# The last steps of a layer-norm, block-FP4 FFN and long-convolution kernel: one silu moved ahead of two squares, and four output tiles handed between engines

## The chip, the cores and the metric

The kernel runs on one NeuronCore of a Trainium2 chip. Its engines are TensorE (PE, matmuls and transposes), VectorE (DVE), ScalarE (ACT), GpSimd (POOL) and SyncE (SP, which only issues transfers). The metric is the device time of one execution in microseconds (us), lower is better. An execution is "faster" or "slower" here only beyond a few tenths of a per cent of about 588 us.

## The reference

The input `u` has 8 sequences of 1024 rows of 256 channels. What is computed is

```python
xn = layernorm(x)                      # x = u, over the 256 channels
s  = causal convolution of xn with a 128-tap kernel per channel + xn * D
gate = fp4(xn) @ fp4(w_gate).T         # 256 -> 704, blocks of 16 share a scale
y    = fp4(xn) @ fp4(w_up).T
h    = silu(gate) * y
g    = silu(fp4(h) @ fp4(w_down).T)    # 704 -> 256
out  = x + s * g
```

where `fp4` rounds every block of 16 to eight magnitudes times the block's own scale and multiplies back.

## The kernel before, in words

The 8192 rows are 64 tiles (NT) of 128 rows, worked two at a time: a pair of tiles is a step, and there are NP = 32 steps. For each tile PE multiplies the normalised input with the gate and up weights (`gate_up`, L1224), ACT takes the silu of the gate half (`silu_gate`, L615), DVE multiplies it with the up half (`h_mult`, L883). One step later DVE, ACT and POOL quantise the pair's 2 x 704 values of `h`: DVE finds block maxima (L785 or L799), scales (L818), ACT squares (`square`, L630), DVE rounds twice (`round_a` L852, `round_b` L857) and multiplies with the split scales (`h_parts`, L891, semaphore `hl_v`). PE then transposes the rounded tile (`h_transpose`, L1233), ACT copies it out of PSUM (`h_copy`, L610, semaphore `hT_a`), PE multiplies it with the down weights (`down`, L1242 and L1244), and ACT takes the last silu into `gbuf` (`silu_out`, L619, semaphore `g_a`). `down` of a tile waits until the `silu_out` two tiles earlier has been done (`after(pe, g_a, n)`), since both use the same half of a PSUM bank.

The convolution runs on PE between the FFN's matmuls in the steps 8 to 29; its result lies in `yv`, the place of the tensor `xh`. The output is `gbuf * yv + u`. Up to tile 55, POOL multiplies (`gated`, L516, in three parts of the channels per four tiles: one of 128 x 512 elements and two of 128 x 256) and sends the product with an accumulating DMA (`add_out`, L520) into `out`, into which SP has copied `u` beforehand (`copy_input`). The last eight tiles are handled at the end: DVE multiplies the six tiles 56 to 61 at once (L1143), POOL sends them with one accumulating DMA, and for tiles 62 and 63 DVE multiplies (L1143) and adds `u` from an SBUF buffer `u_last` (L1152), and SP stores each with a plain DMA (L453).

All engines run lists written out by hand in program order, with semaphores between engines; nothing is scheduled automatically. Around the end the lists are: ACT ends with `step(NP, ...)`, that is `h_copy(60)`, the two squares of the last pair, `silu_out(59)`, `h_copy(61)`, `silu_out(60)`, `down_scale(31)`, and then `silu_out(61)`, `h_copy(62)`, `h_copy(63)`, `silu_out(62)`, `silu_out(63)`. PE ends with transposes of 60, `down(59)`, transposes of 61, `down(60)`, `down(61)`, transposes of 62 and 63, `down(62)`, `down(63)`. DVE ends with the quantisation of tiles 62 and 63, one after the other (`pieces`), and the output multiplications. The kernel's last waits are SP's for its stores and POOL's for its accumulating DMAs.

Of the kernel before, what the change touches and what calls it, by code (L numbers as in the profile page):

```python
# [12 lines left out]
ALU = mybir.AluOpType  # L13
# [4 lines left out]
P = 128  # L18
SEQS, LSEQ, H = 8, 1024, 256
NT = SEQS * LSEQ // P  # L20
NP = NT // 2
# [48 lines left out]
def build(nc, u, u_rev, D, Lre, Lim, logdt, Wre, Wim, wg, wu, wd, out):  # L70
    kpad = nc.dram_tensor("kpad", (H, 2, 3 * P), F16)
    u_t = u.rearrange("s l h -> (s l) h").rearrange("(t p) h -> p t h", p=P)
    urev = u_rev.rearrange("t p h -> p t h")
    out_t = out.rearrange("s l h -> (s l) h").rearrange("(t p) h -> p t h", p=P)

    with ExitStack() as ctx:
        ctx.enter_context(nc.allow_non_contiguous_dma(reason="a small load of D"))

        def sb(name, shape, dt):
            return ctx.enter_context(nc.sbuf_tensor(name, shape, dt))  # L80

        def sem(name):
            return ctx.enter_context(nc.semaphore(name))

        xh = sb("xh", [P, NQ, 2, NT, C2], F16)
        gbuf = sb("gbuf", [P, NT, H], F32)
# [12 lines left out]
        def carve(words):  # L99
            used[0] += words  # L100
            assert used[0] <= 14336
            return work[:, used[0] - words:used[0]]
# [4 lines left out]
        tpl_words = [carve(4 * 2 * P) for _ in range(2)]  # L107
# [7 lines left out]
        xT_words = carve(4 * H)  # L115
        xT = [xT_words[:, 2 * H * i:2 * H * (i + 1)].bitcast(F16).rearrange("p (t c k) -> p t c k", t=2, c=4) for i in range(2)]
        xin = [v[:, 2 * I:].rearrange("p (t h) -> p t h", t=2) for v in vb]
        u_last = carve(2 * H).rearrange("p (t h) -> p t h", t=2)
        by_blk = [v.rearrange("p (c k) -> p c k", k=BLK) for v in vb]
        d_bf, r_f16 = (rbuf.bitcast(dt).rearrange("p (c k) -> p c k", k=BLK) for dt in (BF16, F16))  # L120

# [98 lines left out]
        cv_h = sem("cv_h")  # L220
# [14 lines left out]
        g_a = sem("g_a")  # L235
        o_in = sem("o_in")
        f_p = sem("f_p")
        f_l = sem("f_l")
        f_y = sem("f_y")
        f_t = sem("f_t")  # L240
        f_st = sem("f_st")
        u_in = sem("u_in")
        f_out = sem("f_out")
# [118 lines left out]
            return groups_before(it + 1) - groups_before(it)  # L362

        PEEL = 4
        FIRST = NT // 4 - 2
        OPEN = [min(it for it in range(NP) if groups_before(it + 1) >= q1 * C2 // G8) for q0, q1 in PARTS]

        @block.sync
        def _(sp):
            def load_x(p, par):  # L370

                after(sp, x_r, p - 1)
                sp.dma_start(xin[1 - par], u_t[:, bass.ds(p * 2, 2), :]).then_inc(x_in[par], 16)

            sp.dma_start(dt, bass.AP(logdt.tensor, logdt.offset, [[0, P], [1, H]])).then_inc(s_small, 16)
            for m, w in enumerate((Lre, Lim)):
                dst = (lre, lim)[m]
                for half in range(2):
                    sp.dma_start(dst[64 * half:64 * half + 64, :], w.rearrange("(n o) -> n o", o=1)).then_inc(s_small, 16)
            for m, w in enumerate((Wre, Wim)):  # L380
                for half in range(2):
                    sp.dma_start(wn[:, m, :, 64 * half:64 * half + 64],
                                 w.rearrange("(t p) n -> p t n", p=P)).then_inc(s_wn, 16)
            sp.wait_ge(s_const, 2)
            sp.dma_start(dk[0:P:FA, :], D.rearrange("(o g) -> o g", g=16)).then_inc(s_d, 16)
            for m, w in enumerate((wg, wu)):
                base = wraw[:, m * RW:(m + 1) * RW].rearrange("p (t k) -> p t k", k=H)
                sp.dma_start(base[:, 0:RT - 1, :], w[0:(RT - 1) * P, :].rearrange("(t p) k -> p t k", p=P)).then_inc(s_w, 16)
                sp.dma_start(base[0:I - (RT - 1) * P, RT - 1, :], w[(RT - 1) * P:I, :]).then_inc(s_w, 16)
            sp.dma_start(wraw[:, 2 * RW:].rearrange("p (t i) -> p t i", t=2),  # L390
                         wd.rearrange("(t p) i -> p t i", p=P)).then_inc(s_w, 16)
            for i in range(4):

                sp.dma_start(gbuf[:, 16 * i:16 * i + 16, :], urev[:, 16 * i:16 * i + 16, :]).then_inc(s_xa[i], 16)
            for p in range(2):
                load_x(p, p)

            sp.wait_ge(k_zero, 1)
            for lo in (0, 2 * P - 1):
                w = P - 1 if lo == 0 else P  # L400
                sp.dma_start(kpad.ap()[:, :, lo:lo + w].rearrange("(p a) b i -> p (a b) i", p=P),
                             zero.bitcast(F16).rearrange("p (r i) -> p r i", i=P)[:, :, 0:w]).then_inc(k_pad, 16)

            load_x(2, 0)
            sp.dma_start(u_last, u_t[:, NT - 2:NT, :]).then_inc(u_in, 16)

            def store_filter():
                sp.wait_ge(k_split, 2)
                for part, src in enumerate((kh, kl)):
                    for a in range(8):  # L410
                        sp.dma_start(
                            bass.AP(kpad, part * 3 * P + P - 1 + 16 * a, [[16 * 6 * P, 16], [6 * P, 16], [1, 16]]),
                            src[a:P:FA, :].rearrange("p (g b) -> p g b", b=16)).then_inc(k_dram, 16)

            def load_t(n, par):

                after(sp, cv_h, n - 1)
                sp.dma_start(tpl[par], bass.AP(kpad, n * (4 * 6 * P), [[1, P], [3 * P, 8], [1, 2 * P]])
                             ).then_inc(t_in[par], 16)

            def copy_input(i):

                rows = LSEQ if i < SEQS - 1 else LSEQ - 2 * P
                sp.dma_start(out[i:i + 1, 0:rows], u[i:i + 1, 0:rows]).then_inc(o_in, 16)

            for it in range(PEEL):
                load_x(it + 3, (it + 1) % 2)
                if it == 2:
                    store_filter()
                copy_input(it)  # L430
            for it in range(PEEL, S_CONV):
                load_x(it + 3, (it + 1) % 2)
                copy_input(it)
            sp.wait_ge(k_pad, 32)
            sp.wait_ge(k_dram, 16 * 16)
            sp.wait_ge(w_ca, 13)
            load_t(0, 0)
            sp.wait_ge(x_hl, 2 * S_CONV + 4)
            load_t(1, 1)
            with sp.Fori(0, PAIRS - 1) as q:  # L440
                for par in range(2):
                    load_x(q * 2 + (S_CONV + par + 3), 1 - par)
                    for k in range(4 - 2 * par):
                        load_t(q * 6 + (4 * par + k + 2), k % 2)
            for it in range(S_TAIL - 2, NP - 3):
                load_x(it + 3, (it + 1) % 2)
                for n in range(2 * groups_before(it) + 2, min(2 * groups_before(it + 1) + 2, H // 4)):
                    load_t(n, n % 2)
            for n in range(2 * groups_before(NP - 3) + 2, H // 4):
                load_t(n, n % 2)  # L450
            for n in range(2):
                sp.wait_ge(f_t, n + 1)
                sp.dma_start(out_t[:, NT - 2 + n:NT - 1 + n, :], gbuf[:, NT - 2 + n:NT - 1 + n, :]).then_inc(f_st, 16)  # L453
            sp.wait_ge(f_st, 32)

        @block.gpsimd
        def _(pool):
# [60 lines left out]
            def add_out(t0, t1):  # L518

                nc.gpsimd.dma_start(out_t[:, t0:t1, :], gbuf[:, t0:t1, :], accum_op=ALU.add).then_inc(f_out, 16)  # L520
# [8 lines left out]
            for m in range(2):  # L529
                rows = uu[:, 16 + 8 * m:24 + 8 * m, :]  # L530
# [7 lines left out]

            todo = [(n, part) for n in range(FIRST) for part in range(len(PARTS))]
            made, sent = [0], [0]  # L540
# [28 lines left out]
                if it >= OPEN[0]:  # L569
                    some_gated(it, 4 if it < OPEN[2] else 8)  # L570
            some_gated(NP, NP)
            pool.wait_ge(f_l, 1)
            add_out(4 * FIRST, NT - 2)
            pool.wait_ge(f_out, 16 * (sent[0] + 1))

        @block.scalar
        def _(act):
# [124 lines left out]
            rows = [(r, r) for r in range(16)] + [(16 + r, 16 * r) for r in range(8)]  # L702
# [60 lines left out]
                step(it, it % 2, True, True, it < NP - 3, True, True, True, cv=groups_of(it), c0=groups_before(it))  # L763
            step(NP - 2, 0, False, True, False, True, True, True)
            step(NP - 1, 1, False, False, False, True, True, True)
            step(NP, 0, False, False, False, False, True, True)
            silu_out(NT - 3, 1, 0)
            for t in range(2):
                h_copy(NT - 2 + t, t, (p_hT, p_hT2)[t])
# [4 lines left out]
        def _(dve):  # L774
            own = Steps(dve, dve_n)
            V = nc.vector
# [133 lines left out]
            rows = [(r, r, 0) for r in range(16)] + [(16 + r, 16 * r, 1) for r in range(8)]  # L910
# [228 lines left out]
            def gate_y(t0, t1):  # L1139

                dve.wait_ge(g_a, t1)
                gc = by_two(gbuf[:, t0:t1, :])
                return V.tensor_tensor(gc, gc, yv[:, :, t0:t1, :].rearrange("p q t c -> p t q c"), ALU.mult)  # L1143

            dve.wait_ge(cv_e, H // G8)
            gate_y(4 * FIRST, NT - 2).then_inc(f_l, 1)
            dve.wait_ge(u_in, 16)
            for n in range(2):
                t = NT - 2 + n
                gate_y(t, t + 1).then_inc(f_y, 1)  # L1150
                dve.wait_ge(f_y, n + 1)
                V.tensor_tensor(gbuf[:, t, :], gbuf[:, t, :], u_last[:, n, :], ALU.add).then_inc(f_t, 1)  # L1152

        @block.tensor
        def _(pe):
# [186 lines left out]
```

## Time and profile before

| | us |
|---|---|
| median of 3 runs | 587.93 (586.70, 587.93, 588.83) |
| the profiled execution | 586.48 |
| its span, first to last instruction | 584.7 |
| DVE / PE / ACT / POOL busy | 544.3 / 473.7 / 407.2 / 198.4 |

Times in the rows are counted from the span's start, so 584.7 is its end. Some 1.8 us of the execution's own time lie outside the span. DVE is busy 93% of the span. The change touches only the last 25 us and some transfers; there all engines wait for each other in turn. The granted clock of TensorE (PEclk) is 1.00 at 2.4 GHz and 0.50 at 1.2 GHz.

### The profile page before, as it was taken

The page shows a single profiled execution, that of the slowest core. Times are in us where ns is not written, and L with a number is a line of the kernel's source. Part 1 is how long each engine was busy: PE and PEld are TensorE (multiplying, and loading weights), DVE is VectorE, ACT ScalarE, POOL GpSimd, SP SyncE. Part 2 cuts the span into 40 slices and gives each one's busy share as a digit, 9 for nine tenths or more (in the row PEclk, how much of TensorE's full clock was granted, in tenths as well). Part 3 has the DMA queues.
Part 4 walks back from the last instruction along what each step waited for, and adds up shares of the span by engine and source line. Part 5 has one row for each costly group of instructions (what it writes and reads, how often), then busy time and mean ns, then how long its engine had stood idle before and what let it go on. Part 6 is the DMA issues. An engine that isn't in the chain of part 4 may idle for free.

```text
span 584.7 us, 13233 instructions
## 1 busy us (share of the span) xinstructions
PE 473.7 (81%) x4956; PEld 331.3 (57%) x4956; DVE 544.3 (93%) x689; ACT 407.2 (70%) x568; POOL 198.4 (34%) x302
## 2 busy tenths in 40 slices
PE   0000356668999999999999999999999999998965
PEld 0000234225555567777777777777777777765654
DVE  6999999989999999999999999999999999998884
ACT  6972866889988876767676767676767666664552
POOL 1094000474555551111111111333333333137870
PEclk9999957989999999999999999999999999999998
DMA  5990012225222335353534353535354535339978
GB/s 173 349 281 1 1 36 90 91 27 163 91 91 91 109 83 159 102 146 108 149 105 142 112 147 103 144 111 146 104 143 114 144 107 148 110 59 154 172 104 132
DMA packets 101186, 70.80 MB, mean 121 GB/s; under 512 B 8848, under 2 KB 100752, under 8 KB 101008
## 3 DMA queue, kind: packets, MB, share of 16 engines
q1 hardware_dynamic: 93072, 61.94, 35.8%
q0 software_dynamic: 8064, 8.13, 9.5%
q8 instruction: 39, 0.64, 0.4%
q14 instruction: 11, 0.09, 0.1%
HBM read 61.28 MB, written 16.91 MB: 134 GB/s over the span
## 4 chain that ended last, share of the span: by engine, by line
PE 57%; DVE 24%; issue 9%; POOL 6%; ACT 3%; DMA 0%; SPq 0%; DVEq 0%; POOLq 0%; ACTq 0%
PE ps L1224 27%; PE ps L1242 10%; PE ps L1244 5%; PE ps L1233 5%; PE ps L1257 4%; PE ps L1261 4%; DVE wgu L944 4%; DVE work L857 2%; DVE sm L799 2%; POOL gbuf L516 2%; DVE work L883 2%; PE ps L1212 2%; DVE work L852 2%; DVE xh L919 1%; DVE xh L912 1%
## 5 line engine op out<-in xcount | busy, mean ns | idle before, releaser
L1224 PE MATMUL ps<-wgu,work 128*128 128x512 f16 (+1 forms) x1152 | 242.7, 366 | 17.1 <-DVE work L883 15.9
L1224 PEld LDWEIGHTS ps<-wgu,work 128*128 128x128 f16 x1152 | 109.9, 99 | 128.0 <-issue 17.5
L615 ACT ACTIVATE work<-ps,con 128x704 f32<-128x704 f32 x64 | 54.2, 847 | 95.1 <-PE ps L1224 95.0
L1242 PE MATMUL ps<-wdh,work 128*128 128x256 f16 x704 | 87.9, 274 | 5.5 <-ACT gbuf L619 4.7
L610 ACT COPY work<-ps 128x1408 f16<-128x1408 f16 x64 | 84.7, 1325 | 2.1 <-PE ps L1233 1.9
L852 DVE SCALAR_TENSOR_TENSOR work<-work 128x960 f32<-128x960 bf16 (+2 forms) x67 | 71.8, 1110 | 1.6 <-ACT work L630 1.5
L1242 PEld LDWEIGHTS ps<-wdh,work 128*128 128x128 f16 x704 | 65.4, 98 | 13.4 <-issue 5.3
L516 POOL TENSOR_TENSOR gbuf<-gbuf,xh 128x256 f32<-128x256 f32 (+1 forms) x42 | 41.0, 1048 | 92.0 <-DVE work L865 77.8
L857 DVE SCALAR_TENSOR_TENSOR work<-work 128x1920 f16<-128x1920 bf16 (+3 forms) x36 | 69.7, 1936 | 1.2
L818 DVE TENSOR_TENSOR work<-work,ps 128x960 f32<-128x960 f32 (+2 forms) x63 | 68.4, 1126 | 1.1
L630 ACT ACTIVATE work<-work 128x960 bf16<-128x960 f32 (+2 forms) x67 | 61.8, 960 | 9.3 <-DVE work L818 8.7
L799 DVE TENSOR_REDUCE sm<-work 128x120 f32<-128x1920 f32 (+2 forms) x32 | 66.4, 2074 | 1.3
L891 DVE TENSOR_TENSOR work<-work,sm 128x1408 f16<-128x1408 f16 (+1 forms) x66 | 54.4, 867 | 11.0 <-POOL sm L498 6.0
L883 DVE TENSOR_TENSOR work<-work,ps 128x704 f32<-128x704 f32 x64 | 56.5, 883 | 5.9 <-ACT work L615 5.8
L483 POOL TENSOR_SCALAR sm<-sm 128x2 int32<-128x2 int32 x31 | 9.5, 307 | 138.3 <-DVE sm L806 138.3
L619 ACT ACTIVATE gbuf<-ps,sm 128x256 f32 (+1 forms) x64 | 30.1, 471 | 35.9 <-PE ps L1244 35.8
L506 POOL TENSOR_TENSOR xh<-gbuf,xh 128x1024 f16<-128x1024 f32 x16 | 38.8, 2447 | 45.9 <-ACT xh L592 37.8
L1233 PE MATMUL ps<-id,work 128*128 128x128 f16 x704 | 49.7, 219 | 5.6 <-DVE work L891 5.5
L1244 PE MATMUL ps<-wdl,work 128*128 128x256 f16 x384 | 53.0, 275 | 0.0
L1233 PEld LDWEIGHTS ps<-id,work 128*128 128x128 f16 x704 | 43.1, 98 | 13.9 <-DVE work L891 8.1
L1257 PE MATMUL ps<-xh,work 128*128 128x64 f16 x768 | 50.3, 192 | 0.0
L1261 PE MATMUL ps<-xh,work 128*128 128x56 f16 x768 | 50.1, 191 | 0.0
(153 smaller groups left out, 675.1 us busy)
## 6 DMA issues: line engine op xcount, KB each, us to landing
work<-kpad SPq DMA_DIRECT2D x64, 512.0 KB, 3.8
work<-L_attn_u SPq DMA_DIRECT2D x33, 256.0 KB, 3.0
gbuf<-u_rev SPq DMA_DIRECT2D x4, 2048.0 KB, 18.6
out<-gbuf POOLq DMA_DIRECT2D x7, 1024.0 KB, 9.5
out<-L_attn_u SPq DMA_DIRECT2D x1, 768.0 KB, 5.5
out<-gbuf POOLq DMA_DIRECT2D x1, 768.0 KB, 8.1
work<-L_ffn_w_down SPq DMA_DIRECT2D x1, 704.0 KB, 6.6
work<-L_ffn_w_gate SPq DMA_DIRECT2D x1, 640.0 KB, 4.7
```

Source lines behind the costliest of these rows:

```text
L610: nc.scalar.copy(hT[par], src).then_inc(hT_a, 1)
L799: own.mark(V.tensor_reduce(bm[:, cols], by_blk[pp][:, cols], AX_X, ALU.max, apply_absolute_value=True))
L818: V.tensor_tensor(v, v, sc, ALU.mult).then_inc(v_v, 1)
L852: own.mark(V.scalar_tensor_tensor(v, d_bf[:, c], C0, v, ALU.add, ALU.subtract))
L857: return V.scalar_tensor_tensor(r_f16[:, c], d_bf[:, c], C0, by_blk[pp][:, c], ALU.add, ALU.subtract)
L883: V.tensor_tensor(vb[par][:, I * t:I * t + I], sg, p_gu[:, I:2 * I], ALU.mult).then_inc(h_v, 1)
L1224: last = T.matmul(p_gu[:, a:b], xT[par][:, t, c, :], wgu[:, part, c % 2, a:b], start=(n == 0), stop=(n == len(todo) - 1))
L1233: last = T.transpose(dst[:, c, :], hilo[par][:, t, c * P:c * P + P], id16[:])
L1242: T.matmul(dst, hT[t][:, c, :], wdh[:, c, :], start=(c == 0), stop=False)
L1244: last = T.matmul(dst, hT[t][:, c, :], wdl[:, c, :], start=False, stop=(c == RT - 1))
L1257: T.matmul(dst, tpl[half][:, 2 * c + tp, 0:P], col[:, xp, :], start=(n == 0), stop=False)
L1261: last = T.matmul(dst1, tpl[half][:, 2 * c + tp, P:2 * P], before, start=False, stop=(n == 2))
```

## The change

Three things are altered.

1. ACT's last step is written out: `silu_out(59)`, `h_copy(61)` and `silu_out(60)` now stand before the two squares of the last pair instead of behind them.
2. POOL's list of `gated` jobs covers tiles 56 to 59 too (FIRST goes from 14 to 15 groups of four tiles), three more multiplications and an accumulating DMA of four tiles instead of the one of six. It no longer waits for a multiplication by DVE.
3. Tiles 60 to 63 are multiplied and summed on DVE, 60 and 61 together, then 62, then 63, each followed by a plain store of SP. `u_last` holds four tiles instead of two. It lies in the place of a convolution buffer and is loaded after the last convolution matmul instead of near the start. `copy_input` leaves out four tiles instead of two.

```diff
-        u_last = carve(2 * H).rearrange("p (t h) -> p t h", t=2)
+        u_last = tpl_words[0].rearrange("p (t h) -> p t h", t=4)
...
-        FIRST = NT // 4 - 2
+        LAST = ((NT - 4, NT - 2), (NT - 2, NT - 1), (NT - 1, NT))
+        FIRST = NT // 4 - 1
...
             load_x(2, 0)
-            sp.dma_start(u_last, u_t[:, NT - 2:NT, :]).then_inc(u_in, 16)
...
-                rows = LSEQ if i < SEQS - 1 else LSEQ - 2 * P
+                rows = LSEQ if i < SEQS - 1 else LSEQ - 4 * P
...
-            for n in range(2):
+            sp.wait_ge(cv_h, H // 4)
+            sp.dma_start(u_last, u_t[:, NT - 4:NT, :]).then_inc(u_in, 16)
+            for n, (t0, t1) in enumerate(LAST):
                 sp.wait_ge(f_t, n + 1)
-                sp.dma_start(out_t[:, NT - 2 + n:NT - 1 + n, :], gbuf[:, NT - 2 + n:NT - 1 + n, :]).then_inc(f_st, 16)
-            sp.wait_ge(f_st, 32)
+                sp.dma_start(out_t[:, t0:t1, :], gbuf[:, t0:t1, :]).then_inc(f_st, 16)
+            sp.wait_ge(f_st, 16 * len(LAST))
...
             some_gated(NP, NP)
-            pool.wait_ge(f_l, 1)
-            add_out(4 * FIRST, NT - 2)
-            pool.wait_ge(f_out, 16 * (sent[0] + 1))
+            pool.wait_ge(f_out, 16 * sent[0])
...
-            step(NP, 0, False, False, False, False, True, True)
+            h_copy(NT - 4, 0)
+            silu_out(NT - 5, 1, 1)
+            h_copy(NT - 3, 1)
+            silu_out(NT - 4, 0, 0)
+            for n in range(2):
+                square(NP, 1, False, True, n)
+            down_scale(NP - 1, 1)
...
-            gate_y(4 * FIRST, NT - 2).then_inc(f_l, 1)
             dve.wait_ge(u_in, 16)
-            for n in range(2):
-                t = NT - 2 + n
-                gate_y(t, t + 1).then_inc(f_y, 1)
+            for n, (t0, t1) in enumerate(LAST):
+                gate_y(t0, t1).then_inc(f_y, 1)
                 dve.wait_ge(f_y, n + 1)
-                V.tensor_tensor(gbuf[:, t, :], gbuf[:, t, :], u_last[:, n, :], ALU.add).then_inc(f_t, 1)
+                V.tensor_tensor(gbuf[:, t0:t1, :], gbuf[:, t0:t1, :], u_last[:, t0 - (NT - 4):t1 - (NT - 4), :], ALU.add
+                                ).then_inc(f_t, 1)
```

What stands at ACT's end before, from the copy of tile 60 on. L610 is `h_copy`, L630 `square`, L619 `silu_out`, L637 `down_scale`:

```order
L610 COPY work<-ps 128x1408 [waits dn_p,hT_p]
L630 ACTIVATE work<-work 128x704 [waits v_v,x_hl,hl_v]
L630 ACTIVATE work<-work 128x704 [waits v_v]
L619 ACTIVATE gbuf<-ps,sm 128x256 [waits dn_p]
L610 COPY work<-ps 128x1408 [waits dn_p,hT_p]
L619 ACTIVATE gbuf<-ps,sm 128x256 [waits dn_p]
L637 ACTIVATE sm<-sm,con 128x2 [waits g_a,p2_v]
```

And in the changed kernel, whose line numbers for ACT are one lower (L609, L629, L618, L636):

```order
L609 COPY work<-ps 128x1408 [waits dn_p,hT_p]
L618 ACTIVATE gbuf<-ps,sm 128x256 [waits dn_p]
L609 COPY work<-ps 128x1408 [waits dn_p,hT_p]
L618 ACTIVATE gbuf<-ps,sm 128x256 [waits dn_p]
L629 ACTIVATE work<-work 128x704 [waits v_v,x_hl,hl_v]
L629 ACTIVATE work<-work 128x704 [waits v_v]
L636 ACTIVATE sm<-sm,con 128x2 [waits g_a,p2_v]
```

The silu of tile 59, the copy of tile 61 and the silu of tile 60 have moved ahead of both squares.

POOL's end before, behind the last scales (L516 is `gated`, L520 the accumulating DMA `add_out`):

```order
L516 TENSOR_TENSOR gbuf<-gbuf,xh 128x4x128
L516 TENSOR_TENSOR gbuf<-gbuf,xh 128x4x64 x2
L516 TENSOR_TENSOR gbuf<-gbuf,xh 128x4x128
L516 TENSOR_TENSOR gbuf<-gbuf,xh 128x4x64 x2
L520 DMA out<-gbuf 128x8x256
L520 DMA out<-gbuf 128x6x256
```

And in the changed kernel (L517 and L521):

```order
L517 TENSOR_TENSOR gbuf<-gbuf,xh 128x4x128
L517 TENSOR_TENSOR gbuf<-gbuf,xh 128x4x64 x2
L517 TENSOR_TENSOR gbuf<-gbuf,xh 128x4x128
L517 TENSOR_TENSOR gbuf<-gbuf,xh 128x4x64 x2
L521 DMA out<-gbuf 128x8x256
L517 TENSOR_TENSOR gbuf<-gbuf,xh 128x4x128
L517 TENSOR_TENSOR gbuf<-gbuf,xh 128x4x64 x2
L521 DMA out<-gbuf 128x4x256
```

Three multiplications now stand between the last two accumulating DMAs, and the last DMA carries four tiles instead of six.

## Rows read from the trace of the kernel before

**Rows 1.** The chain of waits that ended last: start us, us, what (565 to 575 us)
```profile
565.51 0.67 issue
566.18 0.47 ACT gbuf L619
...
572.74 0.63 PE ps L1233 x11
573.39 1.34 ACT work L610
```

**Rows 2.** Timeline of ACT: start us, us, engine, line, operation, tiles, count, [idle before, releaser]
```profile
564.22 0.79 ACT L630 ACTIVATE work<-work 128x704 bf16<-128x704 f32 x1 [2.68 <-DVE work L818]
565.48 0.79 ACT L630 ACTIVATE work<-work 128x704 bf16<-128x704 f32 x1 [0.47 <-DVE work L818]
```

**Rows 3.** Timeline of PE from 561 us to its last matmul
```profile
561.27 0.82 PE L1244 MATMUL ps<-wdl,work 128*128 128x256 f16 x6
561.92 0.78 PE L1233 MATMUL ps<-id,work 128*128 128x128 f16 x11
566.78 1.53 PE L1242 MATMUL ps<-wdh,work 128*128 128x256 f16 x11 [4.08 <-ACT gbuf L619]
...
572.57 1.39 PE L1233 MATMUL ps<-id,work 128*128 128x128 f16 x22
574.77 1.37 PE L1242 MATMUL ps<-wdh,work 128*128 128x256 f16 x11 [0.81 <-ACT work L610]
...
577.84 0.82 PE L1244 MATMUL ps<-wdl,work 128*128 128x256 f16 x6
```

**Rows 4.** Timeline of DVE: the last pair's rounding, and the last instruction
```profile
567.14 0.88 DVE L852 SCALAR_TENSOR_TENSOR work<-work 128x704 f32<-128x704 bf16 x1
...
568.98 0.96 DVE L891 TENSOR_TENSOR work<-work,sm 128x704 f16<-128x704 f16 x2
...
571.70 0.96 DVE L891 TENSOR_TENSOR work<-work,sm 128x704 f16<-128x704 f16 x2
...
579.66 0.43 DVE L1152 TENSOR_TENSOR gbuf<-gbuf,work 128x256 f32<-128x256 f32 x1
```

**Rows 5.** Timeline of POOL, single multiplications and one accumulating DMA
```profile
536.87 2.06 POOL L516 TENSOR_TENSOR gbuf<-gbuf,xh 128x256 f32<-128x256 f32 x2
...
560.67 0.74 POOL L516 TENSOR_TENSOR gbuf<-gbuf,xh 128x256 f32<-128x256 f32 x1
...
562.06 1.29 POOL L516 TENSOR_TENSOR gbuf<-gbuf,xh 128x512 f32<-128x512 f32 x1
...
564.66 1.38 POOL L516 TENSOR_TENSOR gbuf<-gbuf,xh 128x256 f32<-128x256 f32 x1
566.34 1.61 POOL L520 DMA_DIRECT2D out<-gbuf  x1 [0.30 <-POOL gbuf L516]
```

**Rows 6.** DVE's L818: one instruction in the timeline; groups of lines (busy, mean ns | idle)
```profile
564.03 1.42 DVE L818 TENSOR_TENSOR work<-work,sm 128x704 f32<-128x704 f32 x1
...
L818 DVE TENSOR_TENSOR work<-work,ps 128x704 f32<-128x704 f32 x4 | 3.4, 885 | 0.1
```

**Rows 7.** Windows: us, busy (x) of PE, PEld, DVE, ACT, POOL, PEclk, DMA share, GB/s
```profile
562.70:566.78 4.08, 0.00 (x2) 0.03 (x1) 3.91 (x8) 2.09 (x4) 3.78 (x4) 1.00 0.05 9
...
567.84:571.24 3.40, 2.74 (x14) 1.67 (x13) 3.30 (x6) 0.67 (x3) 0.11 (x1) 0.50 0.90 104
...
580.10:584.70 4.60, 0.00 (x0) 0.00 (x0) 0.00 (x0) 0.00 (x0) 0.00 (x0) 0.65 0.75 151
```

**Rows 8.** DMA issues (KB each, us to landing), and the landing of SP's two stores
```profile
work<-L_attn_u SPq DMA_DIRECT2D x33, 256.0 KB, 3.0
out<-gbuf POOLq DMA_DIRECT2D x7, 1024.0 KB, 9.5
out<-gbuf POOLq DMA_DIRECT2D x1, 768.0 KB, 8.1
...
DMA to landing us min/median/max: 4.0/4.4/4.8
```

More of the change, by code:

```diff
@@ L237, in build @@
         f_p = sem("f_p")
-        f_l = sem("f_l")
         f_y = sem("f_y")
```

## Prediction, made before the changed kernel ran

> **What bounds the kernel now.** I read the page first: DVE is busy 93% of the span, but the change takes no work from the steady steps. POOL's list up to 566 us, DVE's up to 573 us and PE's whole list are the same, so only the stretch from 562 us on can differ. The second view is the chain of waits at the end [rows 1]. Its last part runs through ACT and PE: a silu at 566.18, the down products of tiles 60 and 61, transposes of 62 and 63, a copy, the down products of 62 and 63, a silu, and DVE's product and sum. The timelines of ACT and PE [rows 2, 3] say why it begins so late. `down(59)` ended at 562.09 (561.27 + 0.82), but ACT had the two squares first in its list. It idled 2.68 us for DVE's L818, squared from 564.22 to 565.01 and from 565.48 to 566.27, and only then came silu 59. PE stood 4.08 us, since `down(60)` needs that silu's half of the bank. DVE meanwhile goes on with its own chain, whose last part is at 572.66 (571.70 + 0.96) [rows 4]. This is the second thing to see: PE starts the last transposes at 572.57. So two chains come to the same point within 0.1 us, one over silu 59 and PE, the other over DVE's rounding of tile 63.
>
> **The moved silu.** With the silus ahead of the squares, silu 59 runs at 562.1 to 562.6, the copy of 61 (1.34 us, as the copy in [rows 1]) at 562.7 to 564.1, `down(60)` from 562.7. At the full clock a down product takes 1.95 us: 574.77 to 578.66 for two [rows 3]. It ends at about 564.7, silu 60 at 565.2, and `down(61)` runs to about 567.3 instead of 572.7. The squares move back: the first from 564.22 to about 565.2, the second ends at 566.8 instead of 566.27. DVE asks for the first at 567.14 [rows 4], so the squares cost nothing; 0.3 us of cover are left for the second's end against even the first rounding. What is late next is DVE: transposes of 63 can't start before its 572.66. Then come 0.70 us of transposes (half of 1.39), `down(62)` and `down(63)`, 3.89 us. Copy 63 (1.34) hides beside `down(62)`. PE would end at 572.7 + 4.6 = 577.3 instead of 578.66. So this edit alone gives at most 1.4 us; the other 4 us are given to an idle PE.
>
> **POOL's three multiplications.** They are new in this place. POOL's accumulating DMA is at 566.34, and work behind such a DMA comes about 1.0 us later and is slow at first: two multiplications took 2.06 us instead of 1.48 there [rows 5]. So POOL asks for the first of the three (128 x 512) at about 567.4 and really works from about 568.0, exactly while DVE rounds tiles 62 and 63. Do they disturb each other? The trace shows it a step earlier. DVE's L818 of 704 elements takes 0.885 us with one operand in PSUM, also beside POOL; at 564.03, with both operands in SBUF and POOL multiplying beside it, it took 1.42 [rows 6]. POOL's multiplication of 256 elements, 0.74 us alone, took 1.38 at 564.66, and ended 0.60 us behind the end of that L818 (566.04 against 565.44) [rows 5]. The reading: one waits for the other, in turns, each for a whole instruction. All eight of DVE's rounding instructions (L852, L857, L891 for each of two tiles) read two operands in SBUF. So each of POOL's three falls between two of them. What DVE loses: for one of 256 elements 1.42 - 0.885 = 0.53 us; for the one of 512, scaled by its length alone, 1.29 - 0.74 + 0.53 = 1.08. Sum 1.08 + 2 x 0.53 = 2.1 us. Bounds: 0 (as beside operands in PSUM) and 1.29 + 2 x 0.74 = 2.8 us. I take 2.1, from the nearest row. DVE's last part then comes at 574.8 instead of 572.66, and that is on the path.
>
> The Trainium skill, "SBUF — State Buffer", section "SBUF: two separate sides", says that VectorE instructions with two SBUF inputs and GpSimd share a pair of ports under an exclusive lock, held for a whole instruction, and that the loser blocks. Rows 5 and 6 agree in kind. By the rule taken to the letter DVE would lose the full 2.8 us, and the sum below would be 0.7 us more.
>
> **PE's clock.** Before, PE stood 4.08 us; the granted clock was still 1.00 then, fell to 0.50 at 567.84, 1.1 us after PE had resumed, and came back at 571.24, 3.4 us later, 4.5 us after PE had resumed [rows 7]. In the changed kernel PE is idle from about 567.3 to 571.5 (transposes of 62, 0.7 us, a little late for POOL), and again to 574.8. That is a longer and emptier stretch than the one before, so I expect the clock at 0.50 when the transposes of 63 start, which is now on the path. At half the clock everything takes twice as long: 9.2 us for transposes and two down products instead of 4.6, and each us at half the clock costs half a us. If it comes back 3.4 us after the start, the cost is 1.7 us. Bounds: 0 (the clock is up) and 4.6 (it never comes back); the row's other reading, 4.5 us, costs 2.25. I take 1.7. PE's last matmul: 574.8 + 4.6 + 1.7 = 581.1, against 578.66 before: +2.4 us.
>
> **DVE's end.** The products of tiles 60 and 61 (512 elements) and their sum come directly behind DVE's last rounding, when silu 61 is long done: some 1.5 us, while PE works; before it was 1.76 us at the same place. They hide. For tile 63 nothing changes: silu, product, sum from 578.66 to 580.09 [rows 3, 4], 1.43 us.
>
> **The stores.** From DVE's last sum to the span's end there are 4.6 us [rows 7], of which the last plain store takes 4.0 [rows 8]. It runs beside POOL's accumulating DMA of 768 KB, issued at 575.4 and landing 8.1 us later, at 583.5; 151 GB/s are moved in that window [rows 7]. Now POOL's last DMA has 512 KB and is issued when its three multiplications are done, at about 572: by the 1.4 us between 1024 and 768 KB it lands after some 6.7 us [rows 8], at 579, before the last store starts. The store of 128 KB then has the queues nearly to itself. Loads of 256 KB land in 3.0 us [rows 8]; I take 2.5 for half the bytes. Bounds 2.0 and 4.0. Gain 1.5 us.
>
> **Other edits.** The load of `u_last` moved behind the convolution is waited for only by DVE at 575, over 30 us later, and SP has nothing queued behind it but stores that come later still. The smaller `copy_input` and the missing early load change nothing anyone waits for. They cost 0: POOL's multiplications of 256 elements at 536.87 [rows 5] wait for the whole convolution, so the load starts before 537 and lands some 3 us later [rows 8]; only a load of over 35 us would make DVE wait.
>
> **Sum** against the profiled execution, span 584.7, 586.48 in all: PE's end +2.4, stores -1.5, together +0.9 us, 587.4. That execution was 1.45 us below the median of 587.93; the timed median is what will be compared, so I forecast 587.93 + 0.9 = 588.8. A change of 0.3%, 1.8 us, is what a measurement here can tell from none; this is inside it.
>
> **Rivals.**
> 1. *The clock stays down.* Same mechanism as mine, but the clock returns only when PE has worked for much longer, say 6.5 us. Then 6.5 / 2 = 3.25 instead of 1.7: 590.4, slower. It decides from 5.2 us at half the clock on (0.9 + 0.9 = 1.8). For it: the return came 4.5 us after PE resumed, with PE busy 2.74 of 3.40 us, and the new stretch starts from an emptier one. Against: once PE resumes it is busy without a break. Chance 0.22.
> 2. *POOL does not hold DVE up*, or waits until DVE is done. Then the 2.1 us go: 586.7 with my clock and stores. If the idle stretch, now only 2.6 us plus 1.9 us around the transposes of 62, also leaves the clock up, 585.0, faster. For it: DVE's instructions follow each other within 0.03 us, and POOL may not get in. Against: it did at 564.66. Chance 0.20, half of it with the faster outcome.
> 3. *The last store is not quicker.* Then the 1.5 us stay: 590.3, slower. It is so if 4.0 us are the store's own time. For it: nothing in the trace stores 128 KB on an idle queue; against: loads of twice that in 3.0. Chance 0.08.
>
> My own case has 0.50 and lies in the no-change band. Faster is 0.11 (half of rival 2 and a little), slower 0.30 (rivals 1 and 3), no change 0.59. The range takes the lower end at 586.0, within rival 2, and the upper at 590.8, above rivals 1 and 3; my own case alone would be 587.7 to 590.0.
>
> **What would show it.** In the changed profile: silu 59 at about 562.1 and PE's 4.08 us wait gone; `down(61)` over by 567.5; POOL's three multiplications between 567.4 and 572, each longer than alone or pushing a DVE instruction to 1.4 us or more; DVE's last L896 (L891 before) ending near 574.8; a granted clock of 0.50 when the transposes of 63 start; less than 3.3 us from the last sum to the end. I am wrong if the last rounding ends at 572.7, if the clock is up at that point, or if the store still takes 4 us.

## The result, and the profile after

| | before | changed |
|---|---|---|
| median of 7 runs, us | 586.92 (586.40 to 588.83) | 589.12 (588.46 to 590.28) |
| profiled execution / its span, us | 586.48 / 584.7 | 589.38 / 587.6 |

The ratio is 1.0033, with a 95% interval of 1.0018 to 1.0048: the change makes the kernel slower by a third of a per cent, 1.9 us. (The medians differ by 2.2 us, the two profiled spans by 2.9.) Run again later beside other kernels, the changed one had 1.0036 (1.0025 to 1.0047). The time forecast was 588.8; its likeliest case, no change that can be told, was just missed. The forecast was counted from 587.93, the median of three runs; seven runs give 586.92.

DVE's timeline of the changed kernel answers to [rows 4]; the last product and sum of tile 63 are at its end (columns: start us, us, engine, line, operation, tiles, count):

```profile
567.09 2.85 DVE L847 TENSOR_SCALAR sm<-sm 128x176 bf16<-128x176 f32 x1
569.97 0.75 DVE L851 SCALAR_TENSOR_TENSOR sm<-sm 128x176 f16<-128x176 f32 x1
570.64 1.41 DVE L857 SCALAR_TENSOR_TENSOR work<-work 128x704 f32<-128x704 bf16 x1
...
575.74 0.96 DVE L896 TENSOR_TENSOR work<-work,sm 128x704 f16<-128x704 f16 x2
...
585.02 0.42 DVE L1155 TENSOR_TENSOR gbuf<-gbuf,work 128x256 f32<-128x256 f32 x1
```

Three instructions in a row are long. L847, a scale conversion of 176 elements ahead of the rounding, took 2.85 us; it takes 0.25 us where nobody holds it (566.91 in e2 below). L851 took 0.75 instead of 0.34, L857 1.41 instead of 0.88. The losses are 2.60, 0.41 and 0.53, together 3.54 us. The last rounding ends at 576.70. Before it was 572.66. Of the 4.04 us between them 0.5 us are older: TensorE's clock came back to 1.00 at 128.5 us instead of 127.5, and all that follows is later by 0.5 us.

POOL's timeline beside it, the answer to [rows 5]:

```profile
566.84 1.60 POOL L521 DMA_DIRECT2D out<-gbuf  x1 [0.30 <-POOL gbuf L517]
567.86 3.44 POOL L517 TENSOR_TENSOR gbuf<-gbuf,xh 128x512 f32<-128x512 f32 x3
571.59 1.31 POOL L521 DMA_DIRECT2D out<-gbuf  x1 [0.30 <-POOL gbuf L517]
```

PE's timeline, the answer to [rows 3]:

```profile
565.90 1.36 PE L1246 MATMUL ps<-wdh,work 128*128 128x256 f16 x11 [0.66 <-ACT gbuf L618]
567.10 0.82 PE L1248 MATMUL ps<-wdl,work 128*128 128x256 f16 x6
574.03 1.36 PE L1237 MATMUL ps<-id,work 128*128 128x128 f16 x11 [6.12 <-DVE work L896]
576.75 1.36 PE L1237 MATMUL ps<-id,work 128*128 128x128 f16 x11 [1.36 <-DVE work L896]
577.90 2.56 PE L1246 MATMUL ps<-wdh,work 128*128 128x256 f16 x11
580.25 1.49 PE L1248 MATMUL ps<-wdl,work 128*128 128x256 f16 x6
581.53 1.84 PE L1246 MATMUL ps<-wdh,work 128*128 128x256 f16 x11
583.20 0.82 PE L1248 MATMUL ps<-wdl,work 128*128 128x256 f16 x6
```

The wait of 4.08 us before `down(60)` is gone, and `down(61)` is over at 567.92. In its place stand 6.12 us of waiting for DVE and 1.36 more. The last transposes and products then take from 576.75 to 584.02, 7.27 us, since the granted clock is down, as the windows show (us, busy of PE, PEld, DVE, ACT, POOL, PEclk, DMA share, GB/s; to be read against [rows 7]):

```profile
572.25:576.75 4.50, 1.36 (x11) 1.09 (x12) 4.40 (x8) 1.32 (x1) 0.66 (x1) 0.50 1.24 197
576.75:582.49 5.74, 5.74 (x33) 4.45 (x34) 1.45 (x3) 1.81 (x3) 0.00 (x0) 0.50 0.42 91
585.45:587.60 2.15, 0.00 (x0) 0.00 (x0) 0.00 (x0) 0.00 (x0) 0.00 (x0) 1.00 0.18 61
```

The last of these windows is the gain: 2.15 us from the last sum to the end instead of 4.60 [rows 7]. The last store, L454 at 585.5, landed after

```profile
DMA to landing us min/median/max: 1.7/1.7/1.7
```

instead of 4.0 [rows 8].

### The profile page after: what moved, and what is told of

It reads as the page before. It is cut to its first block, busy times and chain, and to the rows that moved or that the text cites. A ratio compares the mean times of both kernels' runs of the same rounds, so it can differ in the third digit from the quotient of the medians.

```text
span 587.6 us, 13240 instructions
## 1 busy us (share of the span) xinstructions
PE 477.5 (81%) x4956; PEld 333.4 (57%) x4956; DVE 547.3 (93%) x690; ACT 407.4 (69%) x568; POOL 201.1 (34%) x305
## 4 chain that ended last, share of the span: by engine, by line
PE 56%; DVE 26%; issue 9%; POOL 6%; ACT 2%; DMA 0%; SPq 0%; DVEq 0%; POOLq 0%; ACTq 0%
PE ps L1228 27%; PE ps L1246 9%; PE ps L1248 5%; PE ps L1237 5%; PE ps L1261 4%; PE ps L1265 4%; DVE wgu L949 4%; DVE work L862 2%; DVE sm L804 2%; DVE work L857 2%; POOL gbuf L517 2%; DVE work L888 2%; PE ps L1216 2%; DVE xh L924 1%; DVE work L896 1%
## 5 line engine op out<-in xcount | busy, mean ns | idle before, releaser
L609 ACT COPY work<-ps 128x1408 f16<-128x1408 f16 x64 | 84.9, 1326 | 10.5 <-PE ps L1237 10.3
L517 POOL TENSOR_TENSOR gbuf<-gbuf,xh 128x256 f32<-128x256 f32 (+1 forms) x45 | 44.4, 1084 | 92.0 <-DVE work L870 77.9
L857 DVE SCALAR_TENSOR_TENSOR work<-work 128x960 f32<-128x960 bf16 (+2 forms) x67 | 72.3, 1117 | 1.6 <-ACT work L629 1.5
L629 ACT ACTIVATE work<-work 128x960 bf16<-128x960 f32 (+2 forms) x67 | 61.7, 960 | 6.1 <-DVE work L823 5.5
L1237 PE MATMUL ps<-id,work 128*128 128x128 f16 x704 | 51.6, 224 | 13.0 <-DVE work L896 12.9
L1237 PEld LDWEIGHTS ps<-id,work 128*128 128x128 f16 x704 | 44.4, 100 | 21.9 <-DVE work L896 16.1
L618 ACT ACTIVATE gbuf<-ps,sm 128x256 f32 (+1 forms) x64 | 30.2, 472 | 35.4 <-PE ps L1248 35.3
```

The costliest lines, as they stand in the source:

```text
L609: nc.scalar.copy(hT[par], src).then_inc(hT_a, 1)
L857: own.mark(V.scalar_tensor_tensor(v, d_bf[:, c], C0, v, ALU.add, ALU.subtract))
L1237: last = T.transpose(dst[:, c, :], hilo[par][:, t, c * P:c * P + P], id16[:])
```

## Experiments

The experiments ran in three groups, each beside 23 to 25 runs of the kernel before. Ratios are to those.

| run | what it is | ratio (95%) | median us |
|---|---|---|---|
| e1_act_only | before + moved silus | 0.9982 (0.9967 to 0.9997) | 586.79 |
| e2_no_act | changed, silus in old order | 0.9996 (0.9986 to 1.0007) | 587.52 |
| e3_dve_mult | changed, 56 to 59 multiplied by DVE | 0.9966 (0.9953 to 0.9980) | 585.53 |
| e4_mult_then_dma | changed, multiplications ahead of the DMA | 0.9988 (0.9978 to 0.9998) | 586.98 |
| e5_wait_tile62 | changed, multiplications later | 0.9992 (0.9980 to 1.0004) | 587.43 |
| e7_after_fill | changed + filling matmuls | 0.9993 (0.9978 to 1.0007) | 586.46 |
| e8_all_dve | all eight tiles by DVE, plain stores | 0.9980 (0.9966 to 0.9994) | 586.00 |
| e9_all_dve_fill | e8 + filling | 0.9942 (0.9923 to 0.9962) | 584.01 |
| e10_dve_mult_fill | e3 + filling | 0.9938 (0.9922 to 0.9955) | 583.94 |
| e11_dve_mult_old_act | e3, silus in old order | 0.9963 (0.9948 to 0.9979) | 584.84 |
| after_again | changed | 1.0036 (1.0025 to 1.0047) | 589.35 |

**e1_act_only**, the silus alone:

```diff
-            step(NP, 0, False, False, False, False, True, True)
+            h_copy(NT - 4, 0)
+            silu_out(NT - 5, 1, 1)
+            h_copy(NT - 3, 1)
+            silu_out(NT - 4, 0, 0)
+            for n in range(2):
+                square(NP, 1, False, True, n)
+            down_scale(NP - 1, 1)
```

> Only the ACT part of the change: silu 59, copy 61 and silu 60 ahead of the two squares; POOL, DVE and the stores as before. My theory (the moved silu shifts the end onto DVE's last rounding, and leaves PE idle): PE's 4.1 us wait is gone, DVE's last rounding stays at 572.7, the transposes of 63 start there, PE ends at 577.3 at the full clock or up to 580 if the granted clock is 0.50 for 3.4 to 5 us then. POOL's DMA of six tiles is issued about 0.7 us earlier and lands 8.1 us later, so the span ends between 583.5 and 586: -1 to +1 us against before. Rival (the silu is a plain gain of 1.4 us): the clock is 1.00 when the transposes of 63 start, PE ends at 577.3, and the span is 1 us or more shorter.

The edit alone gains 0.2%, 1.1 us, but PE does not end sooner:

```profile
574.23 1.35 PE L1239 MATMUL ps<-id,work 128*128 128x128 f16 x11 [1.93 <-DVE work L897]
575.38 2.56 PE L1248 MATMUL ps<-wdh,work 128*128 128x256 f16 x11
...
580.35 0.82 PE L1250 MATMUL ps<-wdl,work 128*128 128x256 f16 x6
```

DVE's last rounding ended at 574.17, in time but for the 1.5 us by which this run was later already at 140 us. PE ended at 581.17, 6.94 us after the transposes began and, with the 1.5 us taken off, 1.0 us later than before. The theory holds for PE; the rival's clock of 1.00 was not there. What is gained comes from the end: the last store, at 582.6, landed after 2.3 us instead of the 4.0 of [rows 8]. It started 1.6 us ahead of the landing of POOL's accumulation instead of 3.4:

```profile
DMA to landing us min/median/max: 2.3/2.3/2.3
```

**e2_no_act**, the changed kernel with e1's lines turned back:

> The changed kernel with ACT's last step in its old order, so only the POOL, DVE and store parts. Theory: PE works on the down products of 60 and 61 until about 573 and has its clock back, DVE's last rounding is held up by POOL by 3.5 us as in the changed kernel (ends near 576.2 plus any earlier shift), the transposes of 63 start at a clock of 1.00, and PE ends 4.6 us later, at 580.8. The last store takes 1.7 us. So the time is 2 to 3 us below the changed kernel's, near before's. Rival (the moved silu gains by itself, and the loss is all POOL's): no faster than the changed kernel, up to 1.4 us slower.

It is 0.4% below the changed kernel. PE's last group:

```profile
576.36 0.79 PE L1231 MATMUL ps<-id,work 128*128 128x128 f16 x11 [1.93 <-DVE work L890]
...
580.04 0.82 PE L1242 MATMUL ps<-wdl,work 128*128 128x256 f16 x6
```

4.50 us from 576.36 to 580.86, at a clock of 1.00, against 7.27. PE waited 1.93 us for DVE here too, so with DVE held up by POOL the old order is in time for the last transposes. In the changed kernel the moved silus therefore win nothing and cost 2.77 us: they take PE's work away from the time just ahead of the last products. DVE is held for 2.37 + 0.54 + 0.41 = 3.3 us, of the 3.5 expected, and the long instruction is now the one behind the conversion:

```profile
566.91 0.25 DVE L841 TENSOR_SCALAR sm<-sm 128x176 bf16<-128x176 f32 x1
567.20 2.71 DVE L845 SCALAR_TENSOR_TENSOR sm<-sm 128x176 f16<-128x176 f32 x1
```

The accumulating DMA beside them, with the three multiplications directly behind it in POOL's list:

```profile
566.67 1.60 POOL L521 DMA_DIRECT2D out<-gbuf  x1 [0.30 <-POOL gbuf L517]
```

**e3_dve_mult**, POOL's multiplications taken away (the line that makes the semaphore `f_l` is left out):

```diff
-        FIRST = NT // 4 - 1
+        FIRST = NT // 4 - 2
...
-            pool.wait_ge(f_out, 16 * sent[0])
+            pool.wait_ge(f_l, 1)
+            add_out(4 * FIRST, NT - 4)
+            pool.wait_ge(f_out, 16 * (sent[0] + 1))
...
+            gate_y(4 * FIRST, NT - 4).then_inc(f_l, 1)
             dve.wait_ge(u_in, 16)
```

> The changed kernel, but tiles 56 to 59 are multiplied by DVE at the end, as before the change, and POOL only sends their accumulating DMA of 512 KB; tiles 60 to 63 with plain stores stay. Theory (POOL's three multiplications beside DVE's rounding are the loss): DVE's last rounding is back at 572.7, the transposes of 63 start there, PE ends between 577.3 (clock 1.00) and 580 (0.50 at first). POOL's DMA is issued at about 574.2 and lands by 581.5. Span 581.5 to 584, time 1 to 3 us below before and 3 to 5 us below the changed kernel. Rival (the four-tile handling or the late clock is the loss, not POOL): the time stays within 1 us of the changed kernel's.

0.7% below the changed kernel, some 4 us, and the rival falls. DVE's last rounding ended at 572.84, with 0.18 us of it from earlier, so there is no delay:

```profile
571.88 0.96 DVE L899 TENSOR_TENSOR work<-work,sm 128x704 f16<-128x704 f16 x2
572.76 1.82 DVE L1151 TENSOR_TENSOR gbuf<-gbuf,xh 128x1024 f32<-128x1024 f32 x2
```

PE still needed 7.15 us from 572.90 on, 5.48 of them at the half clock.

**e4_mult_then_dma** and **e5_wait_tile62** move POOL's three multiplications. e4 puts them ahead of the DMA of tiles 48 to 55:

```diff
-                    if all(m // 2 != n // 2 for m, _ in todo):
+                    if all(m // 2 != n // 2 for m, _ in todo) and n < FIRST - 2:
...
             some_gated(NP, NP)
-            pool.wait_ge(f_out, 16 * sent[0])
+            pool.wait_ge(f_p, made[0] - 3)
+            add_out(4 * FIRST - 12, 4 * FIRST - 4)
+            pool.wait_ge(f_p, made[0])
+            add_out(4 * FIRST - 4, 4 * FIRST)
+            pool.wait_ge(f_out, 16 * (sent[0] + 2))
```

> The changed kernel, but POOL's three multiplications of tiles 56 to 59 stand ahead of the accumulating DMA of tiles 48 to 55 instead of behind it. In the changed kernel DVE's small L847 (0.25 us before) took 2.85 us there, far longer than any of POOL's multiplications. Theory (a POOL multiplication that is queued behind an accumulating DMA holds DVE up from the moment the DMA is issued): here no DVE instruction is held longer than 1.3 us and the whole delay of DVE's last rounding is 2.1 us or less instead of 3.5. Time about 1 to 1.5 us below the changed kernel's. Rival (only the multiplications' own length counts, 1.29 + 2 x 0.74 us and some per turn, wherever they stand): the delay stays at 3 to 3.5 us. The DMA of eight tiles goes out 3 us later, so the last accumulation lands near 581.

e5 makes them wait for tile 62:

```diff
+            pool.wait_ge(hl_v, NP)
             some_gated(NP, NP)
```

> The changed kernel, but POOL waits with its three multiplications until DVE has finished tile 62, about 3.6 us behind the issue of the accumulating DMA. Theory (queued directly behind the DMA, the first multiplication holds DVE from before it runs): here the three fall into the rounding of tile 63, no DVE instruction is held longer than 1.3 us, and the delay of DVE's last rounding is 1.7 to 2.1 us instead of 3.5. The rounding of tile 62 is not delayed at all. Time 1 to 1.8 us below the changed kernel's. Rival (every POOL multiplication costs DVE its full length and more, wherever it stands): delay 3 to 3.5 us, time as the changed kernel's.

DVE in e4, where the three run back to back from 567.40 to 570.10:

```profile
567.70 1.10 DVE L843 TENSOR_TENSOR sm<-sm 128x88 f32<-128x88 f32 x1
568.84 0.67 DVE L851 TENSOR_SCALAR sm<-sm 128x176 bf16<-128x176 f32 x1
569.54 0.76 DVE L855 SCALAR_TENSOR_TENSOR sm<-sm 128x176 f16<-128x176 f32 x1
570.22 0.88 DVE L861 SCALAR_TENSOR_TENSOR work<-work 128x704 f32<-128x704 bf16 x1
```

And in e5, first beside the DMA and then beside the three, in the rounding of tile 63:

```profile
568.96 0.25 DVE L848 TENSOR_SCALAR sm<-sm 128x176 bf16<-128x176 f32 x1
569.25 0.34 DVE L852 SCALAR_TENSOR_TENSOR sm<-sm 128x176 f16<-128x176 f32 x1
...
573.15 1.86 DVE L863 SCALAR_TENSOR_TENSOR work<-work 128x704 f16<-128x704 bf16 x1
575.04 1.91 DVE L897 TENSOR_TENSOR work<-work,sm 128x704 f16<-128x704 f16 x2
```

```profile
568.72 1.60 POOL L521 DMA_DIRECT2D out<-gbuf  x1 [0.30 <-POOL gbuf L517]
572.40 4.17 POOL L517 TENSOR_TENSOR gbuf<-gbuf,xh 128x512 f32<-128x512 f32 x3 [2.08 <-DVE work L897]
```

The delays are 0.85 + 0.42 + 0.42 = 1.7 us in e4 and 0.97 + 0.95 = 1.9 us in e5, against 3.54 in the changed kernel and 3.3 in e2. The comparison that tells is e5 with e2: 0.53 us behind the DMA's start DVE began the same instruction in both, and it took 0.34 us in e5 (569.25) and 2.71 us in e2 (567.20), where a multiplication is queued directly behind the DMA. The conversion itself does not tell them apart: at 0.24 us behind the DMA's start it took 0.25 us in e5 and in e2, and at 0.25 us behind it was held in the changed kernel. The rival, that the multiplications cost 3 to 3.5 us wherever they stand, falls.

The runs are 0.5% (e4) and 0.4% (e5) below the changed kernel, about 2.7 and 2.5 us, more than the 1 to 1.8 us expected. DVE's part of that is 1.9 and 1.6 us. The rest is the clock: it was back 3.5 and 3.3 us after the transposes of 63 had begun instead of 5.7, and PE's last group took 6.19 and 6.09 us instead of 7.27.

**e7_after_fill** fills the idle PE of the changed kernel:

```diff
+            pe.wait_ge(cv_e, H // G8)
             for t in range(2):
+                for _ in range((50, 8)[t]):
+                    T.matmul(ps[:, 3328:3584], id16[:], wdh[:, 0, :], start=True, stop=True)
                 pe.wait_ge(hl_v, NP + t)
```

> The changed kernel with idle PE filled: 50 matmuls of 128x256 (constant operands, into a part of PSUM that nobody reads) ahead of the transposes of tile 62, and 8 ahead of those of 63. Nothing else differs. Theory (the moved silu empties PE before the last transposes, and they and the last two down products then run at a granted clock of 0.50): the clock is 1.00 when the transposes of 63 start and PE ends 4.5 to 4.6 us later instead of 7.3. Time 2 to 2.7 us below the changed kernel's. Rival (the last products are slow for another reason, as waiting for copies): they keep 7 us, and the time is the changed kernel's or above it.

```profile
569.95:583.10 13.15, 11.78 (x116) 9.95 (x113) 10.56 (x14) 3.61 (x4) 4.51 (x5) 1.00 0.89 141
```

The window goes from the first filling matmul to PE's end: the clock stays at 1.00. From the start of the last transposes (578.60) to 583.10 there are 4.50 us instead of 7.27, 2.77 us won by 58 matmuls whose result nobody reads. The ratio falls by 0.4%, 2.4 us.

**e10_dve_mult_fill** and **e11_dve_mult_old_act** start from e3: e10 fills PE with 20 and 12 matmuls, and e11 puts the silus back in the old order.

> The kernel of e3_dve_mult (POOL without the three multiplications) with 20 filling matmuls ahead of the transposes of 62 and 12 ahead of those of 63. Theory: the transposes of 63 start about 0.1 us behind DVE's last rounding at a clock of 1.00, PE ends 4.6 us later instead of 7.15. Time 2 to 2.5 us below e3_dve_mult, 4 to 4.5 us below before. POOL's accumulation of 512 KB lands near 580.8, the last store near 581, so the span may not go below 581.2. Rival: the filling delays the transposes by as much as the clock gives back, time as e3_dve_mult.

> The kernel of e3_dve_mult with ACT's last step in its old order (squares first, silu 59 and 60 behind them), so only the store part of the change is left: four tiles with plain stores, four with POOL's accumulation, multiplied by DVE. Theory: PE works through to 572.7 and has its clock back by then, so its end is as before, 4.6 us behind the start of the last transposes, and the stores still land 2.3 us sooner. Span 582 to 582.5 plus any earlier shift; time 5 us below the changed kernel's, and about 1 us BELOW e3_dve_mult, though one edit meant to help is taken out. Rival (the moved silu is a gain once POOL is out of the way): 1 us or more above e3_dve_mult.

e10 is 0.28% below e3, 1.6 us, less than the 2 to 2.5 expected; its last store took 2.7 us beside POOL's accumulation, which landed at about the same time. e11 comes out as e3 does (0.9963 and 0.9966), not 1 us below; only the single profile has PE's end 0.95 us earlier (579.10 against 580.05). The two agree that the moved silus are worth nothing while PE's clock falls, but the expected advantage of the old order is not shown by the times.

**e8_all_dve** and **e9_all_dve_fill** drop the accumulation of tiles 56 to 59 and the copy of the last sequence ahead of it, and DVE multiplies and sums all eight last tiles (`u_last` holds eight tiles; those lines are left out here):

```diff
-        LAST = ((NT - 4, NT - 2), (NT - 2, NT - 1), (NT - 1, NT))
-        FIRST = NT // 4 - 1
+        LAST = ((NT - 8, NT - 4), (NT - 4, NT - 2), (NT - 2, NT - 1), (NT - 1, NT))
+        FIRST = NT // 4 - 2
...
-                rows = LSEQ if i < SEQS - 1 else LSEQ - 4 * P
+                if i == SEQS - 1:
+                    return
```

> The changed kernel, but DVE multiplies and sums all eight last tiles (56 to 59, 60 and 61, 62, 63) and SP stores them plainly; POOL has neither the three multiplications nor a last accumulating DMA, and nothing of the last sequence is copied beforehand. Theory: DVE's last rounding is undelayed, 1024 and 512 elements of product and sum cost 1.2 + 1.2 + 0.7 + 0.7 = 3.8 us behind it, which is just inside the 5.5 us or more until silu 62 at the half clock. No accumulation is under way at the end, so the last store takes 1.7 us. Span as e3_dve_mult or 0.1 lower. Rival (the extra DVE work pushes the last tiles out): 1 us or more above e3_dve_mult.

> e8_all_dve with 20 and 12 filling matmuls ahead of the last two groups of transposes, the version that the theory holds for best. PE ends 4.5 us behind the start of the last transposes; in e10_dve_mult_fill the last store still took 2.73 us beside POOL's accumulation, here 1.7. DVE's 3.8 us of products and sums end 3.8 us behind its last rounding, some 0.5 us later than silu 62, but well ahead of silu 63. So up to 1 us below e10_dve_mult_fill. Rival: tile 62's product and sum, pushed back, push those of tile 63 too: no gain over e10.

e9's profile is as expected: the clock at 1.00, PE's end at 577.38, the last sum at 578.81, and a span of 581.0, the shortest of all:

```profile
572.74 1.22 DVE L1149 TENSOR_TENSOR gbuf<-gbuf,xh 128x1024 f32<-128x1024 f32 x1
574.00 1.23 DVE L1156 TENSOR_TENSOR gbuf<-gbuf,work 128x1024 f32<-128x1024 f32 x1
...
578.38 0.42 DVE L1156 TENSOR_TENSOR gbuf<-gbuf,work 128x256 f32<-128x256 f32 x1
```

Its times do not show a gain over e10: three runs at 582.7 to 582.9 and three at 585.1 to 585.5. e8 is not below e3 either (0.9980 against 0.9966, the intervals overlap), so its times settle neither the expectation nor its rival. The profiles of e4, e5, e7 and e10 have a dip of the clock near 535 us, which makes all that follows 0.9 us later, and those of e5 and e7 one near 135 us worth 1.2 us more; e9's profile has neither. e9's three longer runs have a mean granted clock of 0.968 to 0.971, the three shorter ones of 0.973 to 0.977, so dips may well part them; without a trace of a longer one this is not shown. e9 and e10 both beat the kernel before by 0.6%.

**after_again**, the changed kernel beside these:

> The changed kernel once more, beside the others on one chip: ratio to before between 1.002 and 1.005, DVE's last rounding delayed by 3.5 us, the transposes of 63 at a granted clock of 0.50, the last store 1.7 us. If the ratio is 0.999 to 1.001 here, the small loss belongs to the chip or the hour and not to the kernel.

Everything came as in the first profile: L847 at 2.86 us, PE's last group 7.21 us at a clock that came back at 582.40, a last store of 1.7 us. The loss belongs to the kernel.

## Why the prediction was right, step by step

All steps were there; three sizes were too small. Two of them made the loss 2.5 us larger than forecast, the third took 0.95 us back. That 588.8 lies so near 589.12 is in part luck: the change itself was forecast as +0.9 us and came out as 1.9 by the ratio and 2.9 in the profiled execution, but it was added to a median that lay 1.0 us above that of seven runs. And the likeliest case, no change that can be told, did not come.

| term of the sum | forecast, us | measured, us |
|---|---|---|
| moved silus, at the full clock | -1.4 | -1.45 (worked out: 572.66 + 0.05 + e7's 4.50 = 577.21 for 578.66) |
| DVE held by POOL | +2.1 | +3.54 |
| PE at the half clock | +1.7 | +2.77 |
| last store and end | -1.5 | -2.45 |
| sum | +0.9 | +2.4, and 0.5 from near 125 us |

*The moved silus.* The working was right: the squares ended at 567.11 and DVE never waited for them; the limit became DVE's last rounding. But in the changed kernel the -1.45 us is not theirs. e2, with the silus in the old order, also ended 4.50 us behind the start of its last transposes: once POOL holds DVE for over 3 us, PE is in time either way. What the moved silus add there is the idle PE, that is, the term of the clock.

*POOL's multiplications.* That they hold DVE up is shown by e3: without them DVE is undelayed. Where they do it was partly wrong. The prediction had them fall between the eight rounding instructions, for reading two operands in SBUF; of the three that were held only L857 is one of the eight. L847 and L851 are the scale conversions ahead of them, and L847 reads one tensor, as does e4's L851, held for 0.42 us. The step that was mis-sized is the price of the one of 512, "scaled by its length alone", 1.08 us; with 0.53 for each of 256 it made 2.1, and its upper bound was 2.8. The two of 256 cost 0.41 and 0.53. The one of 512 cost 2.60: it was queued behind the accumulating DMA, and DVE stood from 0.25 us behind that DMA's start, 0.77 us ahead of the multiplication's own recorded start. e4 and e5 put the same three elsewhere, and there the term is 1.7 and 1.9 us, near the 2.1. The nearest row, two multiplications behind a DMA that took 2.06 us instead of 1.48 [rows 5], could not warn of it: DVE's two L818 beside them, with an operand in PSUM, took 0.89 and 0.88 us, their usual time. I read the row as a late start of POOL; that DVE can be held in that time with operands in SBUF, only the new place showed.

The rule of the Trainium skill, "SBUF — State Buffer", section "SBUF: two separate sides", on an exclusive lock fits in kind: in the changed kernel, e2, e4 and e5 DVE waits and POOL works by whole instructions, in turn. It was told too narrowly in the prediction: the section names instructions in a two-port mode beside those with two SBUF inputs, and no run here shows whether L847 is one. The 2.8 us that the prediction took from it, the sum of the multiplications' lengths, is above e4 and e5 and below the changed kernel; the measurements decide.

*The clock.* Right in kind and shown by e7, too small: I let it return 3.4 us after the transposes began, and it took 5.74. The other reading in my text, 4.5 us, would have been nearer. Rival 1 asked for 5.2 us or more; it was the one that came to pass, and with it the verdict slower, to which I had given 0.30. It took both excesses: with the hold as forecast the sum would be 1.0 us, with the clock as forecast 1.3, both under the 1.8. The rows before could not have given this size: counted in the same way, the return took from 3.3 us (e5) to 5.7 us (changed) in kernels that differ in POOL's list alone.

*The stores.* Right, and too small: 1.7 us for 128 KB on idle queues instead of the 2.5 I took, below my lower bound of 2.0. Rival 3 is out. POOL's accumulation landed at 578.6 (571.59 + 7.0), as forecast.

Rival 2 is out as well: POOL got in.

## What to carry to other kernels

Taking a wait off an engine is worth what the next engine in line leaves of it, and near the end of a kernel it can leave TensorE idle and halve its clock for the very products that end the run; look at what PE does in the time ahead of them, and fill it if need be. Work given to GpSimd is not free because GpSimd is idle: ask which DVE instructions on SBUF run beside it, with one tensor operand as well as with two, and keep a GpSimd multiplication from standing directly behind a DMA that GpSimd issues. A final store should not share the queues with an accumulation.

## What was not expected of the hardware

- A DVE instruction of 0.25 us was held for 2.60 us when POOL had a multiplication queued behind its accumulating DMA: in the changed kernel from 0.25 us behind the DMA's start, 0.77 us ahead of the multiplication's recorded start, until 0.2 us after its end. In e2 the same instruction at 0.24 us behind the DMA's start ran freely and the next, at 0.53 us, was held for 2.37 us; in e5, with nothing queued behind the DMA, neither was held. Where in the DMA's issue the hold begins, and why, stays open.
- The clock stayed at 0.50 for 10.24 us in the changed kernel (572.25 to 582.49), 5.74 us of it with PE busy throughout; in e1, e3, e4 and e5 it did so for 6.83 us. From the start of the transposes of 63 to its return there were 5.7 us in the changed kernel, 5.5 in e3, 5.1 in e1, 3.5 in e4 and 3.3 in e5.
- A plain store of 128 KB took 1.7 us with nothing else under way, 2.7 beside the end of an accumulation (e10) and 4.0 in the middle of one [rows 8].
